# Up and gate weights of two chunks in one 512 KB load, in a buffer of two pairs

## The reference, cut to what matters

```python
def reference(x, cond_2048, ...):
    x = x + attn(interpolate(x, cond_2048), wq, wk, wv, wo)
    # a GRU over 512 time steps, batch 4, width 512; its input is x
    hs = gru(cond_2048, x, W_ih, W_hh, b_ih, b_hh)
    # experts: shared (704 hidden units) and 16 of 352 each, top 2 by a sigmoid gate
    y = mlp(hs, sw1, sw2, sw3)
    for e in range(16):
        y = y + mlp(hs, w1[e], w2[e], w3[e]) * weight_of(e)
    return x + y

def mlp(x, w1, w2, w3):
    return (silu(x @ w1.T) * (x @ w3.T)) @ w2.T
```

## Time and profile before

| | us |
|---|---|
| median of 3 runs | 2666.49 (2666.04 to 2667.47) |
| the profiled execution | 2672.57 |
| its span, first to last instruction | 2670.8 |
| PE busy in it | 2549.0 |
| DVE busy | 1891.5 |
| POOL busy | 1113.7 |
| ACT busy | 1047.8 |
| up loads | 400 of 256 KB |
| down loads | 400 of 128 KB |

### The profile page before, as it was taken

The page is one execution under the profiler, slowest core; times in us unless marked ns, Lnnn a source line. Parts: engine busy times, 40 slices in busy tenths (PEclk is TensorE's granted clock), DMA queues, the critical chain, the costliest instruction groups (busy, mean ns, idle before and its releaser), DMA issues.

```text
span 2670.8 us, 159404 instructions
## 1 busy us (share of the span) xinstructions
PE 2549.0 (95%) x69506; PEld 1988.6 (74%) x69506; DVE 1891.5 (71%) x7091; ACT 1047.8 (39%) x3585; POOL 1113.7 (42%) x2940
## 2 busy tenths in 40 slices
PE   7798987879999999999999999999999999999999
PEld 3333443458887888888888888888888888888888
DVE  5766766546667777777788777778777777878622
ACT  5455553443333333333333333333333333333333
POOL 3213111013333555455455545555554555455454
PEclk9899998899999999999999999999999999999999
DMA  4100000000112333333233333323332333233344
GB/s 173 41 18 18 18 2 2 2 34 30 49 49 67 95 93 101 90 98 95 85 103 96 97 95 94 96 85 100 95 93 86 106 95 95 89 89 87 93 148 131
DMA packets 146187, 209.41 MB, mean 78 GB/s; under 512 B 16464, under 2 KB 86352, under 8 KB 145232
## 3 DMA queue, kind: packets, MB, share of 16 engines
q1 hardware_dynamic: 144336, 195.01, 24.2%
q10 hardware_dynamic: 1152, 4.19, 0.4%
HBM read 185.51 MB, written 13.63 MB: 75 GB/s over the span
## 4 chain that ended last, share of the span: by engine, by line
PE 71%; DVE 3%; POOL 1%; issue 1%; ACT 1%; DMA 0%; DVEq 0%; POOLq 0%; ACTq 0%
PE ps L1233 27%; PE ps L1268 25%; PE ps L1283 12%; PE ps L1245 6%; PE ps L1257 2%; POOL hidf L925 1%; DMA w<-in_w 0%; DVE fresh L1127 0%; DVE turn_n L1114 0%; DVE hcur L1132 0%; DVE hcur L1129 0%; DVE turn L1117 0%; DVE npre L1120 0%; ACT cand L1021 0%; POOL hid L937 0%
## 5 line engine op out<-in xcount | busy, mean ns | idle before, releaser
L1233 PE MATMUL ps<-whh,hcur 128*32 128x128 f16 x49152 | 792.1, 220 | 25.3 <-DVE hcur L1132 12.7
L1233 PEld LDWEIGHTS ps<-whh,hcur 128*32 128x32 f16 x49152 | 694.3, 97 | 148.8 <-DVE hcur L1132 119.2
L1268 PE MATMUL ps<-hb,w 128*128 128x256 f16 x6400 | 782.5, 273 | 1.1 <-DMA w<-in_w 1.1
L1268 PEld LDWEIGHTS ps<-hb,w 128*128 128x128 bf16 x6400 | 602.3, 98 | 98.2 <-DMA w<-in_w 2.8
L917 POOL COPY hb<-hcur 128x32 f16<-128x32 f16 x512 | 169.7, 331 | 666.2 <-DVE hcur L1132 666.2
L1014 ACT ACTIVATE r<-ur 128x16 f32<-128x16 f32 x512 | 110.6, 216 | 831.0 <-DVE ur L1108 831.0
L1283 PE MATMUL ps<-hid,w 128*128 128x256 f16 x3200 | 428.3, 273 | 2.2 <-POOL hid L937 1.8
L1283 PEld LDWEIGHTS ps<-hid,w 128*128 128x128 bf16 x3200 | 312.3, 98 | 39.7 <-issue 3.0
L925 POOL TENSOR_TENSOR hidf<-up 128x256 f32<-128x256 f32 x400 | 291.8, 730 | 98.2 <-POOL hid L937 50.7
L937 POOL TENSOR_TENSOR hid<-hidf,hid 128x256 f16<-128x256 f32 x400 | 269.1, 673 | 62.8 <-ACT hid L1010 62.8
L1105 DVE STREAM_TRANSPOSE turn<-ps 128x128 f32<-128x128 f32 x512 | 161.9, 316 | 182.5 <-PE ps L1233 173.6
(11 more groups left out here) (154 smaller groups left out, 3029.6 us busy)
## 6 DMA issues: line engine op xcount, KB each, us to landing
w<-in_w SPq DMA_DIRECT2D x400, 256.0 KB, 2.7
w<-in_w SPq DMA_DIRECT2D x400, 128.0 KB, 2.7
gi_scratch<-gis SPq DMA_DIRECT2D x72, 128.0 KB, 1.7
spare<-gi_scratch SPq DMA_DIRECT2D x36, 128.0 KB, 2.8
gi<-gi_scratch SPq DMA_DIRECT2D x36, 128.0 KB, 2.8
x2T<-in_xT SPq DMA_DIRECT2D x4, 1024.0 KB, 7.0
out<-xo ACTq DMA_DIRECT2D x8, 512.0 KB, 4.3
stage<-in_W_hh SPq DMA_DIRECT2D x3, 1024.0 KB, 5.6
```

Source lines behind the costliest of these rows:

```text
L1233: mm = pe.matmul(ps[j * COLS:(j + 1) * COLS, bank, 0:P], hcur[:, k], whh[:, s, k, at:at + P], start=(k + s == 0), stop=(k == KT - 1 and s ...
L1268: mm = pe.matmul(ps[:, UB[u], w * TOK:(w + 1) * TOK], w13[:, u, w, k], hb[:, f % 2, s, k].rearrange("p b t -> p (b t)"), start=(w + k + s ...
```

## The change

The array of up and gate weights is laid out by pairs of chunks: for each of 25 pairs and each partition, the 2 KB of the even chunk and the 2 KB of the odd chunk lie side by side. One load brings a pair: 512 KB, 4 KB for each partition. The buffer `w13` has two places for a pair, 8 KB a partition instead of 4 KB.

`w13_load(n)` now counts pairs, 200 in the run. It waits until both chunks of the pair two before are done (`up_done` at 2n - 2). The two preloads bring pairs 0 and 1, so chunks 0 to 3. In `chunks` an up load is issued in odd chunks only: at odd n, pair n // 2 + 2, which is chunks n + 3 and n + 4. In even chunks the down load stands behind no up load.

PE still waits once for each chunk, now on the semaphore of the pair's place; the second chunk of a pair finds it raised. Its matmuls read the same weights in the same order.

```diff
-        w13 = sb("w13", [P, 2, 2, KT, P], BF16)
+        w13 = sb("w13", [P, 2, 2, 2, KT, P], BF16)
...
             def w13_load(n):
-                need(sp, up_done, n - 1)
-                sp.dma_start(w13[:, n % 2], a["w13"][n % NCH].rearrange("p (w k i) -> p w k i", w=2, k=KT)).then_inc(w13_in[n % 2], 16)
+                need(sp, up_done, 2 * n - 2)
+                sp.dma_start(w13[:, n % 2], a["w13"][n % (NCH // 2)].rearrange("p (c w k i) -> p c w k i", c=2, w=2, k=KT)).then_inc(w13_in[n % 2], 16)
...
                     n = f * NCH + c
-                    if n + 2 < NBLK * NCH:
-                        w13_load(n + 2)
+                    if c % 2 and n + 3 < NBLK * NCH:
+                        w13_load(n // 2 + 2)
                     w2_load(n)
...
                 n, u = f * NCH + c, c % 2
-                pe.wait_ge(w13_in[u], (n // 2 + 1) * 16)
+                pe.wait_ge(w13_in[n // 2 % 2], (n // 4 + 1) * 16)
...
-                            mm = pe.matmul(ps[:, UB[u], w * TOK:(w + 1) * TOK], w13[:, u, w, k],
+                            mm = pe.matmul(ps[:, UB[u], w * TOK:(w + 1) * TOK], w13[:, n // 2 % 2, u, w, k],
...
-    w13 = np.stack(ups, axis=2).reshape(NCH, P, 2 * KT * P)
+    w13 = np.stack(ups, axis=2).reshape(NCH // 2, 2, P, 2 * KT * P).transpose(0, 2, 1, 3).reshape(NCH // 2, P, 4 * KT * P)
```

## The result

The changed kernel takes 2706.72 us (median of 4 runs, 2697.49 to 2711.86), the kernel before beside it 2666.98. The ratio is 1.0148, with a 95% interval of 1.0134 to 1.0161: slower by 1.5%, where 0.1% less had been forecast, and outside the stated range. The profiled execution took 2711.86 us with a span of 2710.1, 39.3 us more than before.

What follows compares the result with a forecast made beforehand. PE was taken as the bound; 2.7 us of weight-load waits removed from the 2670.8 us span, and the median run 6.1 us under the profiled one, gave 2663.8 us, 0.10% less; range 2659 to 2669.

Steps and rivals of the forecast that it cites:

- Lead time, the part that pays: Up loads, line 1268: pairs issued two chunks ahead land in 3.7 to 4.3 us; all seven weight-load waits go, 2.7 us.
- Behind the larger load: Tail, line 1283: odd chunk's w2 load behind the pair lands in 3.7 us, wanted after 4.79; slack 1.1 us, cost 0.
- rival C: Tail: the w2 load behind a pair lands later than 4.79 us; at 5.3 us +12, so 2675.8 us; chance 0.03.
- Even chunks' down load, start, SP's queue: Even chunk's w2 issued a chunk earlier, preloads of 1 MB, four loads in a row on SP: cost 0.
- Rival A: Scan, line 1233: larger weight bursts lengthen PE's instruction stops, 0.05 us a pair, +8.7, so 2672.5 us; chance 0.05.
- Rival B: Scan, line 1233: half as many bursts halve the 13.8 us of instruction stops, -6.9, so 2656.9 us; chance 0.10.
- Rival D: Up loads: 4 KB pieces are cut in two, a pair costs two loads; result unchanged, chance within the forecast's 0.82.

Runs made afterwards that it cites:

- the kernel with four places: Kernel before with four places for a chunk in `w13`, each chunk's 256 KB loaded alone once its place is free; 2668.86 us, ratio 0.9998.
- the kernel without weights: Kernel before without up loads after the first two chunks and down loads after the first 12; 2654.01 us, ratio 0.9931.
- the six kernels: Rows of 384 KB (four places) and 768 KB (changed kernel), each sent when up is done, 1.3 or 3 us later; 2657.2 to 2740.1 us.

## Why the prediction was wrong

The step that failed is the one that left PE's instruction stops as they were: the sum has no term for them, and the range gives them some 2 to 4 us either way. In the scan they grew by 34.9 us (13.8 to 48.7). The bound was read rightly: PE sets the end, and the kernel got longer by about what its waits grew.

**Lead time, the part that pays.** Its parts held: 3.6 us of landing where 3.7 had been taken, no wait for weights anywhere. The gain of 2.7 us is not shown: the kernel with four places removes the same waits and comes out at 0.9998, with 1.0 us more of issue time. The cause of the longest of those waits was not the lead alone either: a third load of SP (line 868 at 1945.81) had gone right behind the up load that PE then waited for.

**Behind the larger load.** The down load lands in 3.6 us (3.7 taken), line 1283 never waits for it, and rival C didn't happen. **Even chunks' down load, start, SP's queue**: no cost of their own on SP, as said. But the step missed what it was about: by losing its wait this load joined the row, 768 KB instead of 640, and with it (and the GRU load behind it) apart 16 us of issue time were gone. I had costed it by who waits for it and not by who waits behind it.

**Rival A** named the mechanism, the place and the row, and was priced at 0.05 us a pair; it measured (48.7 - 13.8) / 169 = 0.21 us a pair, and I gave it a chance of 0.05. Two arguments against it were wrong. "The bytes are the same and the bursts half as many": the loss doesn't go by the bytes moved or by the share of the DMA engines, which fell from 0.33 to 0.29 in the stage shown. By the counts above I take it to go by how long the instruction packets stay out and when they come again. "In the tail, with half again the DMA share, such stops are only 3.0 us": those 3.0 us are not of the weights at all, for they stand in the kernel without weights as well; and PE takes 9 matmuls in 1 us there and 69 in a scan step, so the tail was no measure of it. I had 13.8 us of stops with no releaser in the rows and asked only whether they would change a little; what they came from, the run without weights answers: 0.3 us are left.

**Rival B** was right that these stops can shrink, but not by this change, and they can shrink by more than half: in the kernel with four places 14.8 us go to 0.6 if the row is sent 3 us later.

**Rival D**: the pieces of 4 KB went whole (28,800 packets fewer on q1, 144 for each of 200 loads saved), and against 2 KB pieces in the same load they helped, 2706.7 against 2726.5 us.

The Trainium skill's page "DMA: Bandwidth & Descriptors", section "Queues, rings and completion order", says that a DMA engine takes turns between its queues at the grain of a packet, and counts some 9 to 17 descriptors to a packet. That is not what the profile calls a packet, which is one piece: a load of 128 pieces shows as 144 of them, 9 for each of 16 engines by my estimate, so a packet of the page could be an engine's whole share of a load. The trace agrees in part. Only 11 of 393 instruction packets started 1 to 3 us after a pair's issue, and they come again at the end of the pair (3.2 us), with down loads of the same row still moving; a turn inside a load is hardly to be seen (8 of 155 rows). With two loads of 256 KB in a row, 26 instruction packets started 2 to 3 us after the first one's issue, against 5 with the same pieces in one DMA; but most waited for the second load too. The prediction took "larger packets" to be larger pieces, and 4 KB pieces did no harm. The page gives the formula that the prediction takes from it for DMAs that GpSimd issues; SP's loads come near it here (2.7 and 3.6 us, against 2.6 and 3.2 by the formula). The same page's rule to batch into larger DMAs held for the transfer (512 KB in 3.6 us, 256 KB in 2.7) and cost 1.5% of the kernel.

What stays open: why one DMA of 512 KB in 2 KB pieces costs more (66.7 us) than two of 256 KB in a row (34.1 us; the 26 early packets against 5 point to turns between loads, but no run shows that they make the difference), and what part of the loss is the GRU load's, the stores' and the down loads'. That the moment of the late packet in the scan step is what decides is inferred from the six kernels and the counted times; no run moved the instruction packets themselves, and the trace doesn't show when one was asked for.

The three kernels with the loads at better moments, 2656 to 2657 us, beat both: 0.9940 (0.9925 to 0.9955) with the down load held back, 2.5 us above the run without weights.

## What to carry to other kernels

PE's instructions come by DMA beside the data, and here a large load kept them out until it was through. So look for time marked "issue" inside PE's densest stretches, ask how large a load may be there and what else is sent beside it (a store, a third load), and try other moments for the loads than the one at which the buffer comes free; here the best lay 3 us later and the worst 1.3 us later. A load that SP holds back may end up right ahead of the next one, so read the order and the gaps off the trace. A larger transfer that nobody waits for is no gain, and can be a loss; and a stop whose releaser the profile doesn't know deserves a run that removes its suspect before it gets a small chance.

## What the runs showed of the hardware

In the scan, instruction packets of 16 KB came each 4 us and took some 1.1 us, and PE went on 1.2 to 1.6 us after the end of the one before which it had stopped (37 stops of over 0.5 us). Few started before an up load was through: 12 of 402 from 1.5 to 2.5 us after the issue of 256 KB, whose last piece ended at 2.3 us, and 11 of 393 from 1 to 3 us after the issue of 512 KB, whose last piece ended at 3.2 us. The 6 rows of the changed kernel that met an output store of 512 KB held 7.5 us of stops, the 6 of the kernel before 0.5 us. A wait of 1.3 us put on a transfer that nobody waited for cost 33 us (2706.7 to 2740.1); one of 3 us gained 27. In the changed kernel the output store took 5.5 us to land instead of 4.3.
